# First layer norm folded into the dense weights, with a new order of the attention work

## What is computed

```python
# q, k, v from x @ W_qkv.T, rotated; 16 heads, d_k = 8, S = 2048
scores = q @ k.T / sqrt(8), causal; attn = softmax(scores); out = attn @ v; proj = out @ W_o.T
x = layernorm(x + proj)                          # eps 1e-5, no scale or shift
scale = max(abs(kernel)) / 7
w = clip(round(kernel / scale), -8, 7) * scale
x = layernorm(x + (x @ w + bias + (x @ a) @ b))
```

## Time and profile before

| what | value |
|---|---|
| median of 3 runs | 441.87 us (441.48 to 441.9) |
| profiled execution, device time | 441.07 us |
| its span, first to last instruction | 439.3 us |
| mean granted TensorE clock | 0.981 |
| TensorE / VectorE / ScalarE / GpSimd busy | 412.0 / 380.5 / 313.5 / 119.5 us |

### The profile page before, as it was taken

How to read it: one execution, slowest core, us unless ns; L and a number is a source line. 1 busy time by engine, 2 the same in 40 slices (tenths; PEclk the granted TensorE clock), 3 DMA queues, 4 the chain that set the end, 5 groups by cost and what they waited for, 6 DMA issues and landing times.

```text
span 439.3 us, 8480 instructions
## 1 busy us (share of the span) xinstructions
PE 412.0 (94%) x3246; PEld 199.0 (45%) x3246; DVE 380.5 (87%) x491; ACT 313.5 (71%) x532; POOL 119.5 (27%) x188
## 2 busy tenths in 40 slices
PE   5989799999899999999999999999999999999983
PEld 2547434443345443455343543344454444445652
DVE  2878789999999999998999999999999976766875
ACT  2454775676865877786878697868787889986850
POOL 8979511202112111212101222011003002135553
PEclk9999789999999999999999999999999999999995
DMA  7522212210000000021200022200000000000101
GB/s 238 181 98 93 104 60 79 66 38 3 0 1 4 1 1 5 0 77 59 69 2 2 3 70 75 57 2 1 1 1 2 1 2 3 2 3 2 27 25 48
DMA packets 12200, 16.57 MB, mean 38 GB/s; under 512 B 2444, under 2 KB 7324, under 8 KB 12160
## 3 DMA queue, kind: packets, MB, share of 16 engines
q1 hardware_dynamic: 11072, 15.75, 11.3%
q0 software_dynamic: 1088, 0.28, 0.4%
HBM read 10.37 MB, written 5.24 MB: 36 GB/s over the span
## 4 chain that ended last, share of the span: by engine, by line
PE 78%; DVE 11%; ACT 6%; issue 3%; DMA 1%; POOL 1%; POOLq 0%; SPq 0%; DVEq 0%; ACTq 0%
PE ps L1264 28%; PE ps L1250 20%; PE ps L1205 16%; DVE pmax L1026 10%; ACT probs L949 5%; PE ps L1173 3%; PE ps L1273 2%; PE ps L1219 2%; PE ps L1215 1%; PE ps L1179 1%; PE ps L1292 1%; PE ps L1229 1%; DMA x_sb<-in_L_attn_x_dram 1%; PE ps L1296 1%; PE ps L1189 1%
## 5 line engine op out<-in xcount | busy, mean ns | idle before, releaser
L1026 DVE TENSOR_REDUCE pmax<-ps 128x2 f32<-128x1024 f32 (+3 forms) x273 | 319.9, 1217 | 34.8 <-PE ps L1205 19.6
L949 ACT ACTIVATE probs<-ps 128x512 f32<-128x512 f32 (+4 forms) x465 | 281.8, 675 | 80.8 <-PE ps L1250 78.1
L1250 PE MATMUL ps<-qS,kS 64*128 64x512 f32 (+3 forms) x664 | 148.3, 404 | 3.5 <-DVE pmax L1026 2.3
L1264 PE MATMUL ps<-probs,vP 128*9 128x512 f32 (+3 forms) x1328 | 145.8, 520 | 0.1
L1205 PE MATMUL ps<-kS,qS 64*128 64x512 f32 (+3 forms) x640 | 137.9, 415 | 8.4 <-ACT probs L949 2.6
L1250 PEld LDWEIGHTS ps<-qS,kS 64*128 64x128 f32 x664 | 75.4, 186 | 82.5 <-ACT probs L949 38.4
L1205 PEld LDWEIGHTS ps<-kS,qS 64*128 64x128 f32 x640 | 65.2, 186 | 69.0 <-DVE pmax L1026 33.1
L854 POOL TENSOR_SCALAR_AFFINE_SELECT probs<-probs 128x512 f32<-128x512 f32 x64 | 40.6, 639 | 117.3 <-ACT probs L949 117.2
L863 POOL DMA_DIRECT2D qS<-mrows x34 | 19.7, 581 | 153.3 <-DVE mrows L1046 153.3
L1264 PEld LDWEIGHTS ps<-probs,vP 128*9 128x9 f32 x1328 | 21.4, 88 | 43.4 <-issue 28.3
L1219 PEld LDWEIGHTS ps<-causal_x,ident_x 64*128 64x128 f32 x188 | 17.8, 186 | 0.0
(11 more groups left out here) (116 smaller groups left out, 200.4 us busy)
## 6 DMA issues: line engine op xcount, KB each, us to landing
qS<-q_parts SPq DMA_DIRECT2D x52, 64.0 KB
...
qS<-mrows POOLq DMA_DIRECT2D x30, 8.0 KB, 1.8
```

The source lines that it names most:

```text
L949: nc.scalar.activation(probs[:, J % PRING, heads[0]:heads[-1] + 1:3 - len(banks), lo:hi], src, ACT.Exp, scale=float(DK) ** -0.5).then_inc( ...
L1026: nc.vector.tensor_reduce(dst, src, AX.X, ALU.max).then_inc(unit_free, 1)
L1250: last = nc.tensor.matmul(ps[:, bank, at:at + w], kS[rows, b, j // TPC, hp, (j % TPC) * TOK:(j % TPC + 1) * TOK], qS[rows, b, c, hp, lo:hi ...
L1264: last = nc.tensor.matmul(bank_of(("PV", n, 0))[VW * h:VW * h + VC, lo:hi], vP[:, j, HG * g + h, :], probs[:, J % PRING, h, lo:hi], start= ...
```

## The change

**First normalisation folded.** The residual r = x + proj is no longer normalised. The transpose and the dense product take r itself (`res`, `resT`), and the weights are centred: GpSimd builds `centre` = I - 1/128, and in a new unit **K** TensorE multiplies it with the quantised weights, to which the low-rank product and the identity (for the residual) have been added, and VectorE copies the result to `ffn_c`. The mean of r drops out in the product, and the reciprocal deviation is a factor per token. It is applied with the bias, in one fused VectorE instruction for each tile of 128 tokens that reads PSUM: product x rstd + bias. NORM 0 and BIAS are gone, and x1, x1b with them.

**New prices and new order.** The prices in `Course` are replaced, the events of the post phase depend on each other more loosely (POST 4 needs POST 3 alone, POST 5 the deviation), and `TURNS` is another string throughout. A wait for the copy of v stands before the first value step of each chunk.

```diff
-POST_STEPS = (("POST", 2), ("POST", 3), ("RSTD", 0), ("NORM", 0), ("POST", 4), ("POST", 5), ("RSTD", 1), ("NORM", 1))
-OFF_PE = ("NORM", "RSTD", "BIAS")
+POST_STEPS = (("POST", 2), ("POST", 3), ("RSTD", 0), ("POST", 4), ("POST", 5), ("RSTD", 1), ("NORM", 1))
+OFF_PE = ("NORM", "RSTD")
...
-    LOAD, COLUMN, GAP, ENTRY, EXIT = 0.1, 1 / 2400, 0.016, 0.115, 0.08
-    TO_ACT, TO_DVE, TO_PE = 0.29, 0.17, 0.13
+    LOAD, COLUMN, GAP, ENTRY, EXIT = 0.096, 1 / 2400, 0.007, 0.122, 0.082
+    TO_ACT, TO_DVE, TO_PE, ACT_TO_PE = 0.302, 0.181, 0.149, 0.18
+    DVE_FIX, ACT_FIX, M_WORK, O_WORK, PLACED, VFIX = 0.064, 0.05, 0.51, 0.49, 1.25, 0.079
...
-            self.act = max(self.act, end + self.TO_ACT) + 0.09 + len(heads) * left(n, j) / 1200
-            self.give(self.act + self.TO_PE, self.took)
+            self.act = max(self.act, end + self.TO_ACT) + self.ACT_FIX + len(heads) * left(n, j) / 1200
+            self.give(self.act + self.ACT_TO_PE, self.took)
...
 def maxima_time(n, unit):
-    return 0.155 + 2 * width(n, unit) / 960
+    return Course.DVE_FIX + 2 * width(n, unit) / 960
...
 TURNS = (
-    "SSSScdSSOfcgcddVVaeVShcSSSSSbeVceSSSedVVViddeSSSSSSVfdVSieSeegdVSSSSOfeVhdVafgeVVObfcfagbgdfheefcgdgigifffgfegfggghfhg")
+    "SSSSAVadVVccSSSSSSMVbdVVcdSSSSSSecVVddSSfcSSVVOedaeVSgcSSfdSSVbeceSSSVdeVSSgdSSVOeeVVVafObfagdffebgcfefcgdgegffgfgefggg"
+)
...
-            def post_bias(n):
-                (first, end), i = tiles(n), turn(n)[0]
-                pool.wait_ge(normed[n], normed_count(n, 0))
-                nc.gpsimd.tensor_tensor(x1b[i][:, first:end, :], x1[i][:, first:end, :], bias_sb[:, :].rearrange("p (a d) -> p a d", a=1)
-                                        .to_broadcast([128, end - first, D]), ALU.add).then_inc(pool_post[n], 1)
-
             def weight_scale():
+                pool.tensor_scalar(centre[:, :], ident[:, :], 1.0 / D, None, ALU.subtract).then_inc(centre_set, 1)
...
+                if k == 5:
+                    dve.wait_ge(pool_post[n], pool_count(0))
+                    for t in range(first, end):
+                        last = nc.vector.scalar_tensor_tensor(res2[i][:, t, :], bank_of(e)[:, t * TOK:(t + 1) * TOK], rstd[i][:, t:t + 1], bias_sb[:, :],
+                                                              ALU.mult, ALU.add)
+                    last.then_inc(unit_free, 1)
+                    released(dve, e)
...
+            def centred():
+                e = ("K",)
+                dve.wait_ge(unit_done, UNIT[e])
+                nc.vector.tensor_copy(ffn_c[:, :], bank_of(e)[:, 0:D]).then_inc(unit_free, 1)
...
-                nc.tensor.matmul(bank_of(e)[:, 0:D], aT[:, :], b_sb[:, :], start=True, stop=True).then_inc(unit_done, 1)
+                nc.tensor.matmul(bank_of(e)[:, 0:D], aT[:, :], b_sb[:, :], start=True, stop=False)
+                nc.tensor.matmul(bank_of(e)[:, 0:D], ident[:, :], ident[:, :], start=False, stop=True).then_inc(unit_done, 1)
+
+            def centre_rows():
+                e = ("K",)
+                banks_taken(pe, e)
+                released(pe, ("L",))
+                pe.wait_ge(centre_set, 1)
+                nc.tensor.matmul(bank_of(e)[:, 0:D], centre[:, :], ffn_q[:, :], start=True, stop=True).then_inc(unit_done, 1)
...
+                if (n, j) in FIRST_OF:
+                    prep_freed(pe, ("V", j // TPC))
...
                 if k == 4:
-                    pe.wait_ge(normed[n], normed_count(n, 0))
+                    released(pe, ("POST", n, 3))
                 if k == 5:
-                    released(pe, ("L",))
+                    released(pe, ("K",))
...
-                        last = nc.tensor.transpose(to, x1[i][:, t, :], ident[:, :])
+                        last = nc.tensor.transpose(to, res[i][:, t, :], ident[:, :])
                     if k == 5:
-                        last = nc.tensor.matmul(to, x1T[i][:, cols], ffn_q[:, :], start=True, stop=True)
+                        last = nc.tensor.matmul(to, resT[i][:, cols], ffn_c[:, :], start=True, stop=True)
```

More of the change, by code:

```diff
@@ L164, in banks_of @@
 def banks_of(e):
-    return 2 if e[0] in ("A", "SS") else int(e[0] in ("S", "M", "L", "O", "POST") or (e[0] == "PV" and e[2] == 0))
+    return 2 if e[0] in ("A", "SS") else int(e[0] in ("S", "M", "L", "K", "O", "POST") or (e[0] == "PV" and e[2] == 0))
 class Course:
@@ L193, in __init__ @@
         self.over_s, self.loads, self.arrived = (None,) * NG, 0.0, ()
+        self.scaling = 0.0
+        self.placed, self.scaled = (0.0,) * NC, (0.0,) * len(TASKS)
         self.loading()
@@ L220, in operands @@
         if g == 0 and c < PICKED:
-            return FAR if any(x[2] == "E" and x[3] <= c for x in PROLOGUE[self.p:]) else 0.0
+            return FAR if any(x[2] == "E" and x[3] <= c for x in PROLOGUE[self.p:]) else self.placed[c]
         at = max(LOADED.index((g, x)) for x in (c, unit[1] if unit[0] == "keys" else c) if (g, x) in LOADED)
@@ L260, in reduced @@
     def reduced(self, end, work):
-        self.dve = max(self.dve, end + self.TO_DVE) + work
+        self.dve = max(self.dve, end + self.TO_DVE, self.scaling) + work
+        self.scaling = 0.0
         self.give(self.dve + self.TO_PE, self.took)
@@ L339, in take @@
             self.values = self.values[1:]
[L340 removed]
+            end = self.whole(self.VFIX + 0.853 * left(n, j) / CH, ready)
             i = self.probs.index(FAR)
@@ L351, in take @@
             g, c, first, end = TASKS[e[0]]
-            self.aside(0.55 * (end - first) / TPC, 0.6, ready)
+            self.aside(0.55 * (end - first) / TPC, self.O_WORK, ready)
             if g == FINAL[c]:
@@ L379, in take @@
-            step = POST_STEPS.index((kind, k)) + 1
-            if step < len(POST_STEPS):
-                self.due += ((at + (0.25 if "RSTD" in (kind, POST_STEPS[step][0]) else self.TO_PE), POST_STEPS[step][0], n, POST_STEPS[step][1]),)
+                self.scaling = self.scaled[n] if k == 5 else 0.0
+                self.aside((0.55 if k in (2, 4) else 1.0) * share, {2: 0.05 + 0.53 * share, 3: 0.2 + 0.53 * share, 4: 0.05 + 0.53 * share,
+                                                                    5: 0.1 + 0.9 * share}[k], ready)
@@ L382, in take @@
+            if kind == "RSTD":
+                self.scaled = self.scaled[:n] + (at + 0.2,) + self.scaled[n + 1:]
+            if kind == "POST" and k == 4:
+                self.due += ((at, "POST", n, 5),)
+            if kind == "POST" and k == 5:
+                self.due += ((self.dve + 0.25, "RSTD", n, 1),)
+            if kind == "RSTD" and k == 1:
+                self.due += ((at + 0.2, "NORM", n, 1),)
         else:
@@ L408, in schedule @@
     for turn in left_over:
-        course.take(course.offer(turn, int(next(left_over), 17) if turn in "abcdefghi" else None))
+        course.take(course.offer(turn, int(next(left_over), 17) if turn in "abcdefg" else None))
     assert course.a == len(course.A) and course.s == len(course.S) and course.v == len(course.V) and not course.due
@@ L461 @@
 PV_AT = {e[1:3]: i for i, e in enumerate(e for e in SCHEDULE if e[0] == "PV")}
+FIRST_OF = [next(e[1:] for e in SCHEDULE if e[0] == "PV" and e[2] // TPC == c) for c in range(NC)]
 DIAGONAL = {e[1:3]: i for i, e in enumerate(e for e in SCHEDULE if e[0] == "S" and e[3] == 0 and on_diagonal(*e[1:3]))}
-POSTS = [e[1] for e in SCHEDULE if e[0] == "NORM" and e[2] == 1]
+POSTS = [e[1] for e in SCHEDULE if e[0] == "NORM"]
 TASK_END = {n: steps(n) - 1 for n in range(len(TASKS))}
@@ L961, in copy_turned @@
                 act.wait_ge(unit_done, UNIT[e])
-                nc.scalar.copy((onT if k == 2 else x1T)[i][:, lo:hi], bank_of(e)[:, lo:hi]).then_inc(turned_copied, 1)
+                nc.scalar.copy((onT if k == 2 else resT)[i][:, lo:hi], bank_of(e)[:, lo:hi]).then_inc(turned_copied, 1)
             for e in SCHEDULE:
```

122 lines of the change are left out of this document (62 added, 60 removed).

## The result

The changed kernel takes 437.69 us (median of 6 runs, 437.25 to 439.57), the kernel before beside it 441.88 (6 runs, 441.39 to 444.04). The ratio is 0.9908, 95% interval 0.9885 to 0.993: faster by 0.9%. The forecast was 437.4.

The account below looks back on a forecast made before the run. TensorE and VectorE were taken as nearly full, with waits in long score runs at VectorE's pace, then an idle tail. Order -2.2 and tail -2.1 gave -4.3 us: 437.4 us forecast, range 431.2 to 442.4.

Parts of the forecast that it names:

- The tail: From last value step to last normalising step: 12.6 us becomes 10.3, -2.3; with the landing -2.1, bounds -3.2 and -1.0.
- third rival: TensorE's clock stays at 2.4 GHz in the tail, g's product gives back 0.6 us: 436.8 us, chance 0.07.
- The landing: After the last output step: e's 256 KB store, started 0.6 us before the last, may delay landing; 0.2 us added.
- The middle: The order part: score runs -0.5, their columns +1.1, waits -3.3, added products +0.5, in sum -2.2 us.
- wait term: TensorE's waits in score runs, counted by run length at the old order's waits: -3.3 us, bounds 0 and about -10.
- columns: Column time of TensorE's score runs, with units starting on the half just used serialised: 133.8 us becomes 134.9, +1.1.
- products: Identity product beside the low-rank one and the centring product on TensorE: at most 0.25 us each, +0.5 in all.
- the prediction's own test: Score-run waits beyond columns and 0.235 us: near 49 for the forecast, 43 first rival, 53 second, 57 last.
- The fold, outside the tail: Post phases late in the program: net VectorE -3.4 us, worth 0 there because TensorE's stream sets the pace.
- Many waits vanish: First rival: order planned on true maximum prices removes a fifth of score-run waits, -10 for -3.3: 431 us, chance 0.17.
- Only the tail gains: Second rival: engines already ran at true intervals whatever the planner thought, wait term 0: 440.9 us, chance 0.15.
- Slower by single sets: Last rival: forty more single sets cost ScalarE-TensorE hand-offs, deciding from 0.1 us each: 443.9 to 446.9 us, chance 0.11.

Follow-up runs that it names:

- e4: Changed kernel with chunk e's output step on VectorE moved ahead of the last half-chunk g's residual addition; 437.88 us, ratio 0.9901 to the kernel before.
- e2: Kernel before with the new order and new prices but the old post phase (both normalisations and the bias kept); 456.87 us, ratio 1.032.
- e7: Changed kernel, same order, replayed with the old prices, so 708 of 831 units get other PSUM banks; 448.73 us, ratio 1.0161 to the kernel before.
- e9: Changed kernel, same order, PSUM banks chosen again by release times measured in its trace (697 units moved); 451.15 us, ratio 1.0192 to the kernel before.
- e11: Changed kernel with 8 filler transposes on TensorE ahead of the first score unit of task 2; 438.04 us, ratio 0.992 to the kernel before.
- e12: Changed kernel with 20 filler transposes on TensorE ahead of the first score unit of task 2; 438.25 us, ratio 0.9914 to the kernel before.
- e5: Kernel before with the folded normalisation alone, each unit kept on the PSUM bank it has in the kernel before; 440.76 us, ratio 0.9977.
- e10: Kernel before with each of its 111 pairs of score sets cut into two single sets on the same banks; 442.48 us, ratio 1.0018.
- e3: Kernel before, order and code unchanged, with the new prices, which put 670 of 810 units in other PSUM banks; 459.09 us, ratio 1.0388.

## Why the prediction was right, and where not

The total came out within 0.3 us, by terms that are each off and partly cancel; that it is so close is luck. The profiled spans differ by 3.8 us where 4.3 was forecast, and the executions of the changed kernel alone spread over 2.3.

**The tail: mechanism right, size off.** Forecast 12.6 to 10.3, measured 12.57 to 9.09; the bias on GpSimd is gone, fused steps take 0.59 to 0.61 for two as taken. What was mis-sized, in us after the last value step: f's dense product ended at 3.8, put at 4.1 to 4.6; g's at 5.5, put at 6.3 to 6.7. g's was put at 0.6 to 1.19 and took 0.68 at 2.4 GHz (427.76): TensorE reached it 0.51 us after its last work, and the granted clock fell only at 429.5, when nothing was left. The third rival's condition thus came true, inside the forecast's own range. By these terms f's output started at 7.0 and not at 8.0, which is 1.0 of the 1.2 us. The other 0.2 are on VectorE: f's, e's and g's output steps follow each other without a gap (429.90, 430.41, 431.43), and as their recorded durations overlap, e's and f's hold g's back by 1.53 us where 0.6 + 1.11 was taken. Of that wait 0.3 us lies behind the end of g's deviation (431.11), which would hold g's output next. With the landing the sum is -2.5, within the bounds of -3.2 and -1.0 set for both.

**The landing: size off.** +0.2 forecast, +1.0 measured. It ate most of what the tail gained beyond its forecast. e4 excludes e's store as the main cause. What the landing goes with is one packet of 8 KB of a queue of kind "instruction". In the six kernels with the old post phase it comes 3 to 4 us before the end, ahead of the last store (436.1 in the kernel before, whose last store is issued at 436.9), and the landing is 2.46 (2.76 in e2, where e's store stands just ahead). In the eight with the fold it comes in the last 2 us (433.6 in the changed kernel), and the landing is 3.13 to 3.38 without e's store just ahead and 3.46 to 3.79 with it in five: the changed kernel, e7, e9, e11 and e12. e's store just ahead goes with 0.1 us (e4 against the changed kernel) to 0.3 (e2 against before), no more than the spread of 0.3 among those five; the fold without it goes with 0.7 (e5). That the packet does it is a correlation, since no run moved the packet alone.

**The middle: the wait term failed in size.** Forecast -2.2: runs -0.5, columns +1.1, waits -3.3, products +0.5. Counted in the trace of after by the same means, columns are 134.9 and runs 166 as forecast. Waits in score runs are 51.3 us, for 52.8 (the first runs included): -1.5. By length, the 85 runs of 4 or 5 units waited 0.16 each as taken; the 50 short ones 0.09 for 0.05 (4.7 us), the 15 longest 1.6 for 1.53 (24.2, forecast 22.9); the 16 of 6 or 7 units are left with some 8.8, forecast 10.2. So the step that failed is to carry each class's average wait from the old order to the new one. By the prediction's own test (49 for the forecast, 53 if only the tail gains) 51.3 lies nearer to 53. The products cost 1.3 us in e5, not 0.5, of which 0.45 is K's wait for a bank. In the changed kernel it is about as much: 0.4 for the identity product, and 0.85 from K to the next score product, which waits 0.37 for ScalarE. Together -0.5 + 1.1 - 1.5 + 1.3 = +0.4, and the measured middle is -1.2; the 1.6 us left are in the 128-wide work and its waits, counted by no term of mine: outside score runs the middle fell from 178.9 to 178.5 us with the added products in it. What made it fall is open. e5 against the changed kernel gives the order -2.2 in the middle, the fold +1.0.

**The fold, outside the tail: worth 0, nearly right.** Fused steps 4.6 us for 16 as forecast, VectorE -3.2 in e5 for -3.4. It bought nearly nothing before the tail: past its two products, e5 keeps the same 1.3 us behind before from 223 to 394 us, and gains 0.3 by 404. The page shows VectorE -6.0 for the whole change; of the 2.8 more, 1.5 are in the same 273 maxima (319.9 to 318.4), which is no work saved. ScalarE's busy time was to rise by 1 us and is 313.5 both times.

**The rivals.** "Many waits vanish" was wrong: 51.3, not 43. "Only the tail gains" is half right: fold and tail give e5's 440.76, the order the other 3 us. "Slower by single sets" falls with e10: its middle is 2.0 us longer for 111 of them, 0.02 each even with the longer low clock counted in, and 0.1 was the deciding price. What I didn't list, because the order and its prices came together, was that the same order with another deal of banks costs 11 to 17 us. The forecast treated prices as a planner's opinion, harmless by itself ("the engines already ran at true intervals whatever the planner thought"); e3, e7 and e9 show that they also fix the banks, and what that is worth.
